# A graph network's normalising stage: attention rows transposed once, pipeline distances moved, edge weights made early

## The reference

```python
# layer 1, applied twice with a relu between (W1: 128x256, W2: 256x128)
h = x @ W
deg = segment_sum(1, dst) + 1;  dinv = rsqrt(deg);  norm = dinv[src] * dinv[dst]
agg = segment_sum(h[src] * norm[:, None], dst) + h * (dinv * dinv)[:, None] + b
x = layernorm(x + agg2)
# layer 2
att = sigmoid(x[src] @ W_att[:d] + x[dst] @ W_att[d:] + b_att)
aggregated = segment_sum((x[src] @ W_msg + b_msg) * att, dst)
r, z, n = gates of a GRU on aggregated @ W_ih.T and x @ W_hh.T
h_new = (1 - z) * n + z * x
x = layernorm(x + gamma * (h_new - mean) * rsqrt(var + eps) + beta)
```

## Time and profile before

| what | value |
|---|---|
| median of 3 runs | 1913.78 us (1913.1 to 1915.42) |
| profiled execution, own time | 1902.41 us |
| its span | 1900.7 us |
| granted TensorE clock, mean | 0.937 |
| busy: TensorE / VectorE / ScalarE / GpSimd | 1566.2 / 1328.6 / 1230.3 / 1018.8 us |
| chain that ended last | PE 71%, DVE 7%, DMA 6%, issue 6%, ACT 6% |

### The profile page before, as it was taken

One profiled execution on the slowest core, in us unless ns is written; L12 is line 12 of the kernel. 1 busy time (PEld: TensorE's weight loads), 2 busy tenths in 40 slices (PEclk: granted clock), 3 DMA queues, 4 the chain that ended last, 5 costly groups with the idle time before them and its releaser, 6 DMA issues.

```text
span 1900.7 us, 36488 instructions
## 1 busy us (share of the span) xinstructions
PE 1566.2 (82%) x8258; PEld 1092.8 (57%) x8258; DVE 1328.6 (70%) x4475; ACT 1230.3 (65%) x3127; POOL 1018.8 (54%) x1009
## 2 busy tenths in 40 slices
PE   5400499999999976988888889699999999995675
PEld 2200378887777755766766666355555555554454
DVE  7916366676666645666666665488888888886687
ACT  0285366666666633666666666477777777775899
POOL 5000466666666626666666662666666666633453
PEclk8855699999999987999999999799999999998999
DMA  8497466654444434777766665577775444428998
GB/s 262 155 342 264 152 195 193 191 180 138 136 135 138 134 131 129 259 254 255 258 200 200 196 199 180 170 227 230 229 233 157 126 131 129 127 87 289 402 333 304
DMA packets 218928, 382.41 MB, mean 201 GB/s; under 512 B 38959, under 2 KB 41228, under 8 KB 218832
## 3 DMA queue, kind: packets, MB, share of 16 engines
q1 hardware_dynamic: 190272, 342.01, 52.3%
q0 software_dynamic: 28560, 39.34, 9.3%
HBM read 222.75 MB, written 177.81 MB: 211 GB/s over the span
## 4 chain that ended last, share of the span: by engine, by line
PE 71%; DVE 7%; DMA 6%; issue 6%; ACT 6%; POOL 1%; SPq 1%; another core or an unknown queue 1%; DVEq 0%; ACTq 0%; POOLq 0%
PE bank L1337 10%; PE bank L1320 9%; PE bank L1312 9%; PE bank L1387 5%; PE bank L1304 5%; PE bank L1373 4%; PE bank L1375 4%; PE bank L1380 4%; PE bank L1379 4%; PE bank L1377 4%; ACT page L864 4%; PE bank L1356 3%; DMA page<-YT 3%; PE bank L1359 2%; PE bank L1299 2%
## 5 line engine op out<-in xcount | busy, mean ns | idle before, releaser
L668 POOL DMA_INDIRECT gath<-XP,ROWI x294 | 297.0, 1010 | 335.6 <-issue 229.0
L668 POOL DMA_INDIRECT gath<-MT,ROWI x294 | 325.0, 1105 | 206.7 <-PE bank L1387 107.0
L668 POOL DMA_INDIRECT gath<-G,ROWI x294 | 294.1, 1000 | 191.5 <-issue 93.5
L1320 PEld LDWEIGHTS bank<-w_sb,page 128*128 128x128 f32 x1568 | 191.7, 192 | 52.1 <-issue 51.8
L1337 PE MATMUL bank<-gath,onehot 128*128 128x128 f32 x1176 | 162.7, 290 | 70.3 <-issue 40.1
L752 ACT ACTIVATE page<-bank,b_sb 128x512 f32<-128x512 f32 x196 | 123.9, 683 | 113.4 <-PE bank L1312 93.3
L1320 PE MATMUL bank<-w_sb,page 128*128 128x128 f32 x1568 | 192.8, 276 | 5.1 <-issue 5.1
L1337 PEld LDWEIGHTS bank<-gath,onehot 128*128 128x128 f32 x1176 | 144.6, 198 | 78.3 <-issue 62.8
L1312 PE MATMUL bank<-page,w_sb 128*128 128x512 f32 x392 | 185.1, 595 | 0.0
L1063 DVE TENSOR_TENSOR page<-bank,DINV 128x512 f32<-128x512 f32 x98 | 67.8, 691 | 159.2 <-PE bank L1320 134.2
L1092 DVE TENSOR_TENSOR page<-bank,page 128x512 f32<-128x512 f32 x98 | 67.8, 692 | 146.5 <-PE bank L1337 125.0
(11 more groups left out here) (213 smaller groups left out, 3574.2 us busy)
## 6 DMA issues: line engine op xcount, KB each, us to landing
page<-YT SPq DMA_DIRECT2D x196, 256.0 KB, 4.5
MT<-page SPq DMA_DIRECT2D x98, 260.0 KB
XP<-page SPq DMA_DIRECT2D x98, 256.0 KB, 2.2
G<-page SPq DMA_DIRECT2D x98, 256.0 KB
OWN<-page SPq DMA_DIRECT2D x98, 256.0 KB
page<-OWN SPq DMA_DIRECT2D x98, 256.0 KB
YT<-page SPq DMA_DIRECT2D x98, 256.0 KB
page<-AD SPq DMA_DIRECT2D x98, 256.0 KB
```

The costliest lines, as they stand in the source:

```text
L668: nc.gpsimd.indirect_dma_start(gath[k][:, w, 0:width], None, rows, bass.IndirectOffsetOnAxis(ap=ROWI[:, at:at + 1], axis=0), bounds_check= ...
L1320: last = nc.tensor.matmul(bank[6 + k][:, j * D:(j + 1) * D], rows[k][:, j * P:(j + 1) * P], w2_sb[:, h, :], start=(h == 0), stop=(h == 1))
```

## The change

Four things. In `norm`, VectorE's add, statistics and normaliser run two steps behind the aggregation in place of one, and everything after them one step later, the attention add two; ScalarE's square root and its normalising keep their distances. The attention row is no longer transposed per group: VectorE copies its four columns into one wide tile (`AD_ALL`, in the place of DSQ), and after the stage four transposes, one ScalarE copy and four DMAs write the table AD. The attention terms use two banks in turn. In the head, VectorE's degree-of-edge steps come before the window tests, ScalarE's square root is taken at its fourth group, and the edge weights are made before the scale step instead of in it.

```diff
@@ SP, norm
-                if g := group_of(5):
+                if g := group_of(6):
                     sp.dma_start(group_of_table(YT, g), n_T[k]).then_inc(n_yst[k], 16)
-                if g := group_of(7):
+                if g := group_of(8):
                     sp.dma_start(group_of_table(MT, g), n_m[k][:]).then_inc(n_mst[k], 16)
-                if g := group_of(8):
-                    k = g.slot(8)
-                    wait(sp, n_ad, g.done())
-                    sp.dma_start(AD[bass.ds(g.index, 1)].rearrange("a j p -> (a j) p"), ad_row[k]).then_inc(n_mst[k], 16)
             run_pass(sp, norm, 8, unroll=8)
+            sp.wait_ge(n_ad, 1)
+            for q, rows in enumerate(AD_CHUNKS):
+                sp.dma_start(ad_rows[q * P:q * P + rows, :], n_r[0][0:rows, q * P:(q + 1) * P]).then_inc(ad_st, 16)
+            sp.wait_ge(ad_st, 16 * len(AD_CHUNKS))
@@ GpSimd
-            wait_all_dmas(pool, n_mst, 2)
+            wait_all_dmas(pool, n_mst)
@@ ScalarE, scale
-                    if g.fixed and g.index == FREE:
+                    if g.fixed and g.index == U - 1:
                         act.wait_ge(run_steps, 1)
                         nc.scalar.activation(win_q[0:NG], win_deg[0:NG], ACT.Sqrt).then_inc(run_steps, 1)
@@ ScalarE, norm
-                if g := group_of(4):
+                if g := group_of(5):
                     nc.scalar.activation(n_T[k], bank[2 + g.slot(2)][:], ACT.Copy).then_inc(n_trc, 1)
-                if g := group_of(6):
+                if g := group_of(7):
                     nc.scalar.activation(kept(g) if g.kept else n_h[k], bank[6 + g.slot(2)][:], ACT.Copy).then_inc(n_hk, 1)
-                if g := group_of(7):
-                    k = g.slot(4)
-                    wait(act, n_adt, g.done())
-                    wait(act, n_mst[g.slot(8)], g.dma_freed(8, 2))
-                    nc.scalar.activation(ad_row[g.slot(8)], bank[5][0:J, 0:P], ACT.Copy).then_inc(n_ad, 1)
             run_pass(act, norm, 7, unroll=8)
+            act.wait_ge(n_zz, NG)
+            act.wait_ge(n_adt, 1)
+            nc.scalar.activation(n_r[0], bank[3][:], ACT.Copy).then_inc(n_ad, 1)
@@ VectorE, head: the steps from win_eq to win_deg now stand before those from win_loc to held
@@ VectorE, scale: edge_weights() at group FREE + 2 gone; its eight lines stand before the pass
@@ VectorE, norm
-                if g := group_of(1):
+                if g := group_of(2):
                     nc.vector.tensor_tensor(n_z[k], bank[g.slot(2)][:], n_r[k], ALU.add).then_inc(n_zz, 1)
                 if g := group_of(0):
                     ...  (the three one-hots, as before)
-                if g := group_of(6):
+                if g := group_of(8):
+                    both = bank[4 + g.slot(2)][:, 0:2 * J].rearrange("p (j a) -> p j a", j=J)
                     wait(dve, n_mm, g.done())
-                    nc.vector.tensor_tensor(by_tile(n_m[g.slot(8)][:])[:, :, D:DM], bank[4][:, 0:2 * J].rearrange("p (j a) -> p j a", j=J),
+                    nc.vector.tensor_copy(AD_ALL[:, bass.ds(g.index * J, J)], both[:, :, 1:2].rearrange("p j a -> p (j a)"))
+                    nc.vector.tensor_tensor(by_tile(n_m[g.slot(8)][:])[:, :, D:DM], both,
                                             batt_sb[:].unsqueeze(1).to_broadcast([P, J, 2]), ALU.add).then_inc(n_mc, 1)
-                if g := group_of(1):
+                if g := group_of(2):
                     row_stats(g, lambda j: n_z[k][:, j * D:(j + 1) * D], n_s6, n_yy)
-                normaliser(group_of(1), group_of(2), n_s6, n_sd, n_root, n_dq, n_var, n_rs)
+                normaliser(group_of(2), group_of(3), n_s6, n_sd, n_root, n_dq, n_var, n_rs)
@@ TensorE, norm
-                if g := group_of(3):
+                if g := group_of(4):
                         last = nc.tensor.transpose(bank[2 + k][:, j * P:(j + 1) * P], n_m[g.slot(8)][:, j * DM:j * DM + D], ident[:])
-                if g := group_of(7):
-                    wait(pe, n_mc, g.done())
-                    wait(pe, n_ad, g.done() - 1)
-                    nc.tensor.matmul(bank[5][0:J, 0:P], n_m[g.slot(8)][:].rearrange("p (j d) -> p j d", d=DM)[:, :, D + 1:DM]
-                                     .rearrange("p j a -> p (j a)"), ident[:], start=True, stop=True).then_inc(n_adt, 1)
-                if g := group_of(5):
+                if g := group_of(6):
                     nc.tensor.matmul(bank[6 + g.slot(2)][:], whh_sb[:, 2 * D:3 * D], y, start=True, stop=True).then_inc(n_hn, 1)
-                    wait(pe, n_mc, g.done() - 1)
+                    wait(pe, n_mc, g.freed(2))
-                        last = nc.tensor.matmul(bank[4][:, 2 * j:2 * j + 2], y[:, j * P:(j + 1) * P], watt_sb[:], start=True, stop=True)
+                        last = nc.tensor.matmul(bank[4 + g.slot(2)][:, 2 * j:2 * j + 2], y[:, j * P:(j + 1) * P], watt_sb[:], start=True, stop=True)
-            both_ways(norm, 7, unroll=8)
+            both_ways(norm, 6, unroll=8)
+            pe.wait_ge(n_mc, NG)
+            for q, rows in enumerate(AD_CHUNKS):
+                last = nc.tensor.transpose(bank[3][0:rows, q * P:(q + 1) * P], AD_ALL[:, q * P:q * P + rows], ident[:])
+            last.then_inc(n_adt, 1)
```

More of the change, by code:

```diff
@@ L51 @@
 BACK = max(at - P * w for w, (at, n) in enumerate(FAST_COLS))
+AD_CHUNKS = [min(P, NT - at) for at in range(0, NT, P)]
 NOWHERE = 1000.0
@@ L344, in build_gnn @@
         a_x, a_xb, a_s, a_T, a_h0, a_h1, a_g, a_r = names(4, 4, 2, 2, 2, 2, 4, 4)
-        n_r, n_z, n_T, n_h, n_a = names(4, 4, 4, 4, 2)
+        n_r, n_z, n_T, n_h = names(4, 4, 4, 4)
         n_m = pages[18:26]
-        ad_row = [rows[0:J, u * P:(u + 1) * P] for rows in n_a for u in range(4)]
+        AD_ALL = DSQ
         c_y, c_ad, c_h, c_hn, c_a, c_r, c_z, c_t, (c_sq,) = names(4, 4, 4, 4, 2, 2, 2, 2, 1)
@@ L705, in _ @@
                 nc.gpsimd.tensor_scalar(o_t[k], kept(g) if g.kept else o_h[k], bn[:, 5:6], bn[:, 6:7],
-                                    ALU.mult, ALU.add).then_inc(o_q, 1)
+                                        ALU.mult, ALU.add).then_inc(o_q, 1)
         @block.scalar
@@ L775, in norm @@
                     wait(act, n_rs, g.done())
-                    wait(act, n_mst[g.slot(8)], g.dma_freed(8, 2))
+                    wait(act, n_mst[g.slot(8)], g.dma_freed(8))
                     for j in range(J):
@@ L965, in _ @@
             nc.vector.tensor_scalar(win_deg[q], win_deg[q], 1.0, None, ALU.add).then_inc(run_steps, 1)
+            link(nc.vector.tensor_tensor(win_loc[q], win_df[q], per_window(bound_c), ALU.subtract))
+            link(nc.vector.tensor_tensor(win_ok[q], win_loc[q], per_window(inside_c), ALU.is_lt))
+            link(nc.vector.scalar_tensor_tensor(win_ok[q], win_loc[q], 0.0, win_ok[q], ALU.is_ge, ALU.mult))
+            link(nc.vector.tensor_tensor(win_run[q, :, 0:P - 1], win_df[q, :, 0:P - 1], win_df[q, :, 1:P], ALU.is_gt))
+            link(nc.vector.memset(win_run[q, :, P - 1:P], 0.0))
+            nc.vector.tensor_reduce(unsorted[q], in_one_row(win_run, 0, W * P), AX_X, ALU.add)
+            link(nc.vector.tensor_reduce(held[q], in_one_row(win_ok, 0, W * P), AX_X, ALU.add))
+            nc.vector.tensor_tensor(held[q], held[q], unsorted[q], ALU.subtract).then_inc(held_steps, 1)
             link(nc.vector.scalar_tensor_tensor(win_loc[q], win_loc[q], NOWHERE, win_ok[q], ALU.add, ALU.mult))
@@ L999, in _ @@
             nc.vector.memset(e_att[:], 0.0).then_inc(ready, 1)
-            def edge_weights():
-                dve.wait_ge(run_steps, 2)
-                link(nc.vector.reciprocal(win_wd[q], win_q[q]))
-                link(nc.vector.tensor_tensor(win_run[q], win_wd[q], win_wd[q], ALU.mult))
-                link(nc.vector.tensor_tensor(win_run[q], win_run[q], win_deg[q], ALU.mult))
-                link(nc.vector.tensor_scalar(win_run[q], win_run[q], -0.5, 1.5, ALU.mult, ALU.add))
-                nc.vector.tensor_tensor(win_wd[q], win_wd[q], win_run[q], ALU.mult).then_inc(run_steps, 1)
-                dve.wait_ge(run_steps, 4)
-                link(nc.vector.tensor_copy(WD[:, 0:WT], bank[7][:, 0:WT]))
             def scale(group_of):
@@ L1022, in scale @@
                     last.then_inc(s_half, 1)
+            dve.wait_ge(run_steps, 2)
+            link(nc.vector.reciprocal(win_wd[q], win_q[q]))
+            link(nc.vector.tensor_tensor(win_run[q], win_wd[q], win_wd[q], ALU.mult))
+            link(nc.vector.tensor_tensor(win_run[q], win_run[q], win_deg[q], ALU.mult))
+            link(nc.vector.tensor_scalar(win_run[q], win_run[q], -0.5, 1.5, ALU.mult, ALU.add))
+            nc.vector.tensor_tensor(win_wd[q], win_wd[q], win_run[q], ALU.mult).then_inc(run_steps, 1)
+            dve.wait_ge(run_steps, 4)
+            link(nc.vector.tensor_copy(WD[:, 0:WT], bank[7][:, 0:WT]))
             dve.wait_ge(kept_in, 16 * KEPT)
```

25 lines of the change are left out of this document (8 added, 17 removed).

## The result

The changed kernel takes 1896.37 us (median of 4 runs, 1894.37 to 1897.52), the kernel before 1914.6 us in the same rounds (1913.1 to 1918.57): ratio 0.9907, 95% interval 0.9895 to 0.9919. It is 18 us faster; 76 were forecast, and the time lies outside the range. The profiled execution is one of these runs: span 1895.4 us, own time 1897.13. The first profile of before (own time 1902.41) was a quick one of its kind. A second one, of the same kernel but from another job, has a span of 1912.7, and against that the change's 17.3 us lie as follows. All times are read from the starts of instructions: first gather of a stage, first matmul of an aggregation.

The account below looks back on a forecast made before the run. The prediction took a closed TensorE-VectorE loop of 4.66 us a group to bound the normalising stage. Terms -69 (stage), -7 (edge weights), 0 and 0 summed to -76, giving 1838 us from 1913.8; 8-in-10 range 1820 to 1881.

Parts of the forecast that it names:

- The loop (1): Normalising stage: VectorE's add moved back opens the TensorE-VectorE loop, 4.66 us a group becomes 2.33 and bounds nothing.
- What is late next (3): Normalising stage: GpSimd's gathers, 3.90 us a group, limit next and never wait after the restart for group 10; stage -69 us.
- The 2 us given back for a stall of the code: Normalising stage: 2 us taken off the 75.6 us gain for a code stall that both engines keep.
- The 5 us for the transfers: Normalising stage, first half: 5 us taken off the gain because transfers would need 303 GB/s; bounds 0 and 18.
- Rival A: TensorE's late signals keep GpSimd waiting; the step only loses L1350, 4.65 to 4.34; 1879 us, chance 0.21.
- B: The gathers never limit the normalising stage; TensorE stays at 3.73 us a group; 1823 us, chance 0.06.
- C: The loop closes elsewhere, perhaps by ScalarE's root; step stays 4.65, only edge weights count; 1907 us, chance 0.08.
- The attention row (2): Per group, TensorE loses L1350's 0.31 us, bound 4.04 to 3.73; VectorE gains a copy taken as 0.16, covered by slack.
- Later steps (4): Normalising stage: ScalarE's work, transposes, copies and stores moved one or two steps back, and a deeper pass, cost 0.
- the end (5): End of the normalising stage: new transposes, copy and four DMAs cost 0, bounds -1 and +2 us.
- Edge weights (6): Scale stage: weights made early, in VectorE's 44 us of idling, so stores no longer run dry; -7 us, bounds -4 and -8.
- D: VectorE's one-hots stretch GpSimd's gathers, up to 4.95 us a group, so the kernel gets slower; 1934 us, chance 0.05.

Follow-up runs that it names:

- deeper_only: The kernel before with VectorE's add, the transposes, copies and stores one step later, attention row still transposed per group, edge weights late; ratio 1.0015.
- before_again: The kernel before, unchanged, profiled a second time; 1914.47 us.
- before_third: The kernel before, unchanged, run again in a job where signals were on time; 1832.26 us, against 1831.52 in the same job.
- after_again: The changed kernel, unchanged, run again in a job where no signal was over 0.02 us late; 1816.32 us, ratio 0.9918 to before.
- plain_loads: The changed kernel with three plain loads of consecutive rows per group instead of gathers by index in the normalising stage; 1778.74 us, ratio 0.9324 to before.
- row_only: The changed kernel with distances and late edge weights of the kernel before, so only the attention row is collected and transposed at the end; ratio 1.0004 to before.
- weights_only: The kernel before with the edge weights alone made early; ratio 0.9972.
- after: The changed kernel in its first measurement and profile; 1896.37 us, ratio 0.9907 to before.
- eight_later: The changed kernel with eight buffers for gathered rows, GpSimd held to three groups ahead for the normalising stage's first 16 groups; 1899.64 us, ratio 0.9957 to before.
- eight_slots: The changed kernel with eight buffers for gathered rows in the normalising stage instead of four; 1901.23 us, ratio 0.9967 to before.
- the two runs made for that: The changed kernel with a small GpSimd fill before each gather, ratio 0.9956; or each group's third gather waiting for the first two's rows, ratio 1.1096.

## Why the prediction was wrong

- *The loop (1).* Right as arithmetic: the add no longer stands before the next aggregation. Wrong as the bound: the earlier trace rows holds two equal readings, since the add itself starts on a late signal, and that signal is as late as GpSimd's burst makes it. deeper_only opens the loop alone, and its step stays at 4.72. I had written down that TensorE's signals come 1.35 and 0.70 late beside gathers, and then summed as if they would stop with the loop.
- *What is late next (3).* This is the step that failed. "Then should never wait again" assumed that signals come with the matmuls' end. Measured in the changed kernel's profile: 44.1 us of waits in 196, step 4.68 for 3.90, and a stage shorter by 5.9 us (first profile of before, the one of the sum) or 11.4 (second), for 69. What holds it in place is the signal that comes some 0.85 us after the third gather. Where the signals are on time, the same term is right to 0.01 (3.91), but before is at 4.05 there and not at 4.65, so the whole change gains 15 us (0.9918 of 1831.1) and not 76 either. The 2 us given back for a stall of the code that both kernels keep are shown by no run: the step from aggregation 51 is 6.58 in the first profile of before, 4.69 in before_again and 4.04 in before_third. The 5 us for the transfers have no trace either: in after_again the stage's first half steps at 3.91 with 286 GB/s, its second at 3.90.
- *Rival A* named the mechanism, with 0.21; its price was off. It took L1350's 0.31 out of 4.65, though GpSimd's loop holds no L1350: 4.34 for 4.68, 28 us for 6 to 11. Priced by its own loop (3.60 of burst, the delay after it, the restart) it would have given no gain in the step, 1914 - 7 = 1907, against a measured 1896. Its rows spoke against me: the signals were late only beside gathers, and no rule of mine said why they should cease.
- *Rivals B and C.* C, with 0.08, had the step right (4.65 stays) and came nearest in time, 1907 for 1896. Its sentence, that the loop closes elsewhere, is what happened; its reason, ScalarE's square root, was not: the loop closed over GpSimd's wait. B is wrong in either place: with the signals on time GpSimd's 3.91 sets the step, not TensorE's own.
- *The attention row (2).* TensorE's own bound was put at 3.73 and came out at 3.53 (plain_loads), from 4.05 in before_third. Under the hold this is worth nothing on its own (row_only). VectorE's copy takes 0.15 and hides.
- *Later steps (4), the end (5).* (4) holds in place (after_again); alone, in deeper_only, the deeper pass cost 13 us at the stage's end, nearly all of it by the lower clock, where 0 was priced. (5): the last aggregation to the next gathers takes 23.2 for 23.8: -0.5, in the bounds.
- *Edge weights (6).* Right: -5.4 measured (weights_only), -7 predicted.
- *D.* The gathers took 997 ns at the median and at most 1120 in the changed kernel (3 of 294 above 1.06), 1059 in the earlier trace rows. In no run does one take over 1.20. The Trainium skill warns of a lock of the shared port (SBUF — State Buffer, Who interferes with whom). It shows in no run here; whether these one-hots run in a mode that takes it isn't shown either.

## What to carry to other kernels

When a consumer starts later than the end of what it waits for, find the reason before opening the loop that it stands in: a late signal is a resource of its own, and it belongs in the price of every rival. A loop with equal sides explains a step and does not prove it; look for the engine whose restart shares the same signal. And profile the kernel before in more than one place: the same code had another bound there.

## What the runs showed of the hardware

- Three gathers by index in a row on GpSimd (0.99 each, 1.30 apart) held back TensorE and its signals until some 0.85 us after the third; with two gathers and a plain load only signals beside the second gather were late, by 0.23, and with plain loads none was, at a DMA share of 0.97. The delay after the last gather grows with the row: at the median 0.89 after three and 1.33 after six (after), some 1.9 after fifteen and 2.8 after 21 (eight_later, three signals). Longer rows of gathers stopped TensorE for up to 16 us (eight_slots).
- This held in three jobs (and the first measurement) and was absent in two, with the same kernels: before 1907 to 1917 us and 1831, its step 4.73 and 4.05. The five jobs ran on five chips (12, 8 and 3 with the hold, 14 and 9 without); whether it is the chip, or something else that differs from job to job, isn't shown. The second stage took 499 us with the hold and 489 without.
- What in a row of gathers causes it stays open, and so does the way by which GpSimd reaches TensorE: the two runs made for that fell where there was no hold.
